# A cross-attention and expert layer: keys and values ahead of the queries, LayerNorm's constants as two-tensor operations

## What is computed

```python
def _layernorm(x, eps=1e-05):
    m, v = jnp.mean(x, -1, keepdims=True), jnp.var(x, -1, keepdims=True)
    return (x - m) / jnp.sqrt(v + eps)

# cross-attention, 16 heads of 32
q = _layernorm(x) @ Wq + bq
k, v = ctx @ Wk + bk, ctx @ Wv + bv
x = x + softmax(q k^T * SCALE) v @ Wo + bo
# (causal self-attention whose values have width HD - ROPE = 0: it adds nothing)
# expert layer: top 2 of 8 experts for each of the 512 tokens
x = x + moe(_layernorm(x))
```

## Time and profile before

| what | value |
|---|---|
| time, median of 3 runs | 1229.38 us (1228.88 to 1230.99) |
| profiled execution, its own time | 1227.9 us |
| its span, first to last instruction | 1226.1 us |
| mean granted TensorE clock | 0.97 |
| TensorE products busy | 1143.8 us, 93% of the span |
| VectorE busy | 958.2 us, 78% |
| ScalarE busy | 704.6 us, 57% |
| GpSimd busy | 428.0 us, 35% |

### The profile page before, as it was taken

How to read it: one execution, slowest core, us unless ns; L and a number is a source line. 1 busy time by engine, 2 the same in 40 slices (tenths; PEclk the granted TensorE clock), 3 DMA queues, 4 the chain that set the end, 5 groups by cost and what they waited for, 6 DMA issues and landing times.

```text
span 1226.1 us, 23151 instructions
## 1 busy us (share of the span) xinstructions
PE 1143.8 (93%) x7488; PEld 1054.2 (86%) x7489; DVE 958.2 (78%) x2082; ACT 704.6 (57%) x1418; POOL 428.0 (35%) x378
## 2 busy tenths in 40 slices
PE   4899999999999999999999998757889999889998
PEld 4799999999999999999999997635668898668897
DVE  6578888888888888888888888865876756876655
ACT  3456656656656656656656656443575565665654
POOL 5454754754654654654664640010000000000000
PEclk9899999999999999999999999966899999989999
DMA  5322122122122122122122103113755634655633
GB/s 181 101 63 62 40 70 61 38 70 61 38 70 61 38 70 61 38 70 61 39 69 61 58 23 118 50 52 105 244 189 184 206 109 164 221 191 193 201 117 103
DMA packets 74304, 121.15 MB, mean 99 GB/s; under 512 B 10776, under 2 KB 35480, under 8 KB 74272
## 3 DMA queue, kind: packets, MB, share of 16 engines
q1 hardware_dynamic: 74272, 120.73, 30.6%
HBM read 118.62 MB, written 2.10 MB: 98 GB/s over the span
## 4 chain that ended last, share of the span: by engine, by line
PE 79%; DVE 9%; ACT 5%; DMA 3%; issue 3%; DVEq 0%; SPq 0%; ACTq 0%
PE ps L401 18%; PE ps L403 17%; PE ps L402 17%; PE ps L1285 7%; PE ps L1337 7%; PE ps L1321 4%; PE ps L1322 3%; DMA w_raw<-in_w_dram 2%; PE ps L1386 2%; DVE w_lo L1027 2%; DVE mx L955 1%; DVE k_mix L877 1%; PE ps L1429 1%; DVE w_lo L1019 1%; PE ps L1430 1%
## 5 line engine op out<-in xcount | busy, mean ns | idle before, releaser
L545 POOL TENSOR_TENSOR ctx_hi<-ctx_raw,no_query 128x1152 fp32r<-128x1152 f32 x64 | 142.8, 2231 | 290.2 <-PE ps L403 281.2
L877 DVE SCALAR_TENSOR_TENSOR k_mix<-ps,bk_sb,k_mix 64x384 fp32r<-64x384 f32 (+1 forms) x256 | 162.3, 634 | 82.1 <-ACT k_mix L644 77.8
L684 ACT ACTIVATE probs<-ps,negmax 128x1152 f32<-128x1152 f32 x64 | 78.3, 1223 | 201.1 <-DVE negmax L958 201.1
L401 PE MATMUL ps<-wv_hi,ctx_hi 128*128 128x256 f32 (+1 forms) x624 | 181.8, 291 | 6.7 <-DVE k_mix L877 6.5
L549 POOL TENSOR_TENSOR ctx_lo<-ctx_raw,ctx_hi 128x1152 fp32r<-128x1152 f32 x64 | 179.7, 2808 | 5.0
L403 PE MATMUL ps<-wv_hi,ctx_lo 128*128 128x256 f32 (+1 forms) x624 | 175.7, 282 | 0.0
L402 PE MATMUL ps<-wv_lo,ctx_hi 128*128 128x256 f32 (+1 forms) x624 | 174.9, 280 | 0.0
L644 ACT ACTIVATE k_mix<-ps,bk_sb 64x384 fp32r<-64x384 f32 (+1 forms) x256 | 150.8, 589 | 24.0 <-PE ps L403 19.4
L969 DVE TENSOR_TENSOR pt_mix<-ps,pt_mix 128x384 fp32r<-128x384 f32 (+1 forms) x256 | 142.2, 580 | 1.4 <-ACT pt_mix L695 1.4
L401 PE MATMUL ps<-ctx_hi,wk_hi 128*128 128x384 f32 (+1 forms) x384 | 133.2, 347 | 0.0
L403 PE MATMUL ps<-ctx_hi,wk_lo 128*128 128x384 f32 (+1 forms) x384 | 132.3, 345 | 0.0
(11 more groups left out here) (219 smaller groups left out, 2668.5 us busy)
## 6 DMA issues: line engine op xcount, KB each, us to landing
w_raw<-in_w_dram SPq DMA_DIRECT2D x68, 1024.0 KB, 5.3
ctx_raw<-in_ctx_t_dram SPq DMA_DIRECT2D x48, 576.0 KB, 3.8
ctx_raw<-in_ctx_t_dram SPq DMA_DIRECT2D x16, 673.5 KB, 4.1
q_both<-q_scratch SPq DMA_DIRECT2D x14, 128.0 KB, 3.1
x<-in_x_dram SPq DMA_DIRECT2D x1, 1024.0 KB, 5.4
wq_raw<-in_wq_dram SPq DMA_DIRECT2D x1, 1024.0 KB, 7.7
q_scratch<-q_out SPq DMA_DIRECT2D x1, 1024.0 KB, 5.4
wo_raw<-in_wo_dram SPq DMA_DIRECT2D x1, 1024.0 KB, 5.4
```

The source lines that it names most:

```text
L401: pe.matmul(acc_ap, a_hi, b_hi, start=start, stop=False)
L545: nc.gpsimd.tensor_tensor(ctx_hi[slot][:, :, 0:n], ctx_raw[slot][:, :, 0:n], no_query[:].rearrange("p (o i) -> p o i", o=1).broadcast_to([ ...
L877: last = nc.vector.scalar_tensor_tensor(out=k_mix[other, 2 * a + i, cols], in0=ps[rows, bank, 0:m], scalar=bk_sb[rows, a:a + 1], in1=k_mix ...
```

## The change

1. **Order of the opening.** SP issues the three biases first, then wk and ctx chunk 0 in three slices of the contraction (128 rows of wk, the same 128 of ctx), then wv, x, ctx chunk 1, wq. ScalarE and VectorE split each slice as it comes, and unit 0 starts with its first slice (`by_parts`). TensorE does all units of chunks 0 and 1 (0 to 9), then the transposes of xn0, then the queries, then units 10 to 20.
2. **Who splits.** ctx chunk 0: ScalarE high, VectorE low; chunk 1: ScalarE high, GpSimd low; wq_lo moves from VectorE to GpSimd.
3. **LayerNorm in pieces** between the units' halves on VectorE: statistics after unit 0, variance after unit 1, inverse after unit 4, normal rows in two pairs after units 5 and 6. ScalarE waits for the variance between its key and value halves of chunk 0, and splits wq before the halves of chunk 1.
4. **LayerNorm's arithmetic**, in both LayerNorms: eps added from a tile; the factor 0.5 replaced by doubling the reciprocal; `tensor_scalar` on the rows replaced by `scalar_tensor_tensor` with rstd spread over the columns.
5. **First queries** are placed by groups of heads: group 0 under the query products, groups 1 to 3 in pairs of blocks between the halves of chunk 2 (ScalarE) and chunk 3 (VectorE). The store of the queries goes behind two loads of ctx in SP's queue. SBUF is laid out anew to suit.

```diff
+            sp.dma_start(bk_sb[:], bk_t).then_inc(bias_loaded, 16)
+            sp.dma_start(bq_sb[:], bq_t).then_inc(bias_loaded, 16)
+            sp.dma_start(bv_sb[:], bv_t).then_inc(bias_loaded, 16)
+            for k in range(KC):
+                sp.dma_start(wkv_raw[:, 0, k, :], wk[k * P:(k + 1) * P, :]).then_inc(first_loaded[k], 16)
+                sp.dma_start(ctx_raw[0][:, k, 0:KEYS[0]], ctx_view[0, :, k, 0:KEYS[0]]
+                             ).then_inc(first_loaded[k] if k < KC - 1 else ctx_loaded[0], 16)
+            sp.dma_start(wkv_raw[:, 1], wv.rearrange("(k p) n -> p k n", p=P)).then_inc(wv_loaded, 16)
             sp.dma_start(x0[:], x_rows).then_inc(x_loaded, 16)
+            load_ctx(0, 1, 1)
             sp.dma_start(wq_raw[:], wq.rearrange("(k p) n -> p k n", p=P)).then_inc(wq_loaded, 16)
...
             make_norm_tables()
-            for m in range(CHUNKS):
-                split_ctx(m + 1, m, 16 * (m // 2 + 1), UNIT0[m - 1] if m >= 2 else None)
+            pool.wait_ge(ctx_high, 2)
+            pool.wait_ge(ctx_split, 1)
+            nc.gpsimd.tensor_tensor(ctx_lo[1][:, :, 0:KEYS[1]], ctx_raw[1][:, :, 0:KEYS[1]],
+                                    ctx_hi[1][:, :, 0:KEYS[1]].bitcast(F32), ALU.subtract).then_inc(ctx_split, 1)
+            pool.wait_ge(wq_high, 1)
+            nc.gpsimd.tensor_tensor(wq_lo[:], wq_raw[:], wq_hi[:].bitcast(F32), ALU.subtract).then_inc(wq_split, 1)
+            for m in range(2, CHUNKS):
+                split_ctx(m + 1, m, 16 * (m // 2 + 1), UNIT0[m - 1])
...
+            split_first(wkv_raw[:, 1], wv_hi[:], wv_loaded).then_inc(wkv_high, 1)
+            split_first(ctx_raw[1][:, :, 0:KEYS[1]], ctx_hi[1][:, :, 0:KEYS[1]], ctx_loaded[1]).then_inc(ctx_high, 1)
...
             act.wait_ge(bias_loaded, 48)
+            job_high(None, 0, range(len(KEY_UNITS)))
+            act.wait_ge(var_ready, 1)
+            nc.scalar.activation(sd[:], ve[:], ACT.Sqrt).then_inc(sd_ready, 1)
+            warm(ACT.Exp, 1)
+            job_high(None, 0, range(len(KEY_UNITS), UNITS[0]))
+            split_first(wq_raw[:], wq_hi[:], wq_loaded).then_inc(wq_high, 1)
+            job_high(None, 1, range(UNITS[1]))
...
+            for c in range(2, CHUNKS):
+                for k in range(UNITS[c]):
+                    job_high(None, c, [k])
+                    if c == 2 and k < HPG:
+                        for i in (2 * k, 2 * k + 1):
+                            src, to, pairs, cols = first_queries(i, 1, GROUPS)
+                            last = nc.scalar.copy(qbd_hi[to, pairs, cols], q_out[src, 1:GROUPS, 0:NQ])
...
-                    nc.vector.tensor_scalar(dst[:, t, :], src[:, t, :], mv[:, t, 0:1], rstd[:, t:t + 1],
-                                            ALU.subtract, ALU.mult).then_inc(xn_ready, 1)
+            def normal_rows(src, dst, tiles):
+                for t in tiles:
+                    nc.vector.scalar_tensor_tensor(out=dst[:, t, :], in0=src[:, t, :], scalar=mv[:, t, 0:1],
+                                                   in1=rstd[:, t:t + 1].broadcast_to([P, D]), op0=ALU.subtract,
+                                                   op1=ALU.mult).then_inc(xn_ready, 1)
...
+            job_low(None, 0, KEY_UNITS[:1])
+            dve.wait_ge(x_loaded, 16)
+            for t in range(TT):
+                last = nc.vector.bn_stats(stat[:, t, :], x0[:, t, :])
+            step(last)
+            job_low(None, 0, KEY_UNITS[1:])
+            variance()
+            job_low(None, 0, range(len(KEY_UNITS), UNITS[0]))
+            inverse_deviation(1)
+            job_low(None, 1, KEY_UNITS[:1])
+            normal_rows(x0, xn0, range(2))
+            job_low(None, 1, KEY_UNITS[1:])
+            normal_rows(x0, xn0, range(2, TT))
+            job_low(None, 1, range(len(KEY_UNITS), UNITS[1]))
...
+            project(units_of(CHUNKS)[0], 0, PROJ_BANK, by_parts=True)
+            for c in range(2):
+                for k in range(UNITS[c]):
+                    if c > 0 or k > 0:
+                        pe.wait_ge(wkv_split, KC if k in KEY_UNITS else KC + 1)
+                        run_job(None, c, [k])
+            turn(xn0, 0, TT)
+            pe.wait_ge(wq_split, 1)
+            pe.wait_ge(xt_split, KD)
+            pe.wait_ge(proj_split, UNIT0[2])
```

More of the change, by code:

```diff
@@ new lines, in _ @@
+            dve.wait_ge(pv_taken, 1)
+            dve.sem_inc(pv_free, 1)
+            dve.wait_ge(tables_ready, 5)
+            for c in range(2, CHUNKS):
+                for k in range(UNITS[c]):
+                    job_low(None, c, [k])
+                    if c == CHUNKS - 1 and k < HPG:
+                        dve.wait_ge(qbd_high, GROUPS)
+                        for i in (2 * k, 2 * k + 1):
+                            src, to, pairs, cols = first_queries(i, 1, GROUPS)
+                            last = nc.vector.tensor_tensor(qbd_lo[to, pairs, cols], q_out[src, 1:GROUPS, 0:NQ],
@@ L1234, in _, with project @@
             pe.wait_ge(psum_zeroed, 1)
-            turn(xn0, 0, TT)
-            pe.wait_ge(wq_split, 1)
-            pe.wait_ge(xt_split, KD)
-            for m in range(KD):
-                for k in range(KD):
-                    last = three_pass(pe, ps[:, 4 + m, :], wq_hi[:, k, m * P:(m + 1) * P], wq_lo[:, k, m * P:(m + 1) * P],
-                                      xt0_hi[:, k, :], xt0_lo[:, k, :], k == 0, k == KD - 1)
-                last.then_inc(q_ready, 1)
-            def project(unit, n, bank):
+            def project(unit, n, bank, by_parts=False):
                 kind, a, c = unit
                 for k in range(KC):
+                    if by_parts:
+                        pe.wait_ge(wkv_split, k + 1)
+                        if k < KC - 1:
+                            pe.wait_ge(first_split, k + 1)
+                        else:
+                            pe.wait_ge(ctx_split, 1)
                     if kind == "keys":
```

173 lines of the change are left out of this document (93 added, 80 removed).

## The result

The changed kernel takes 1240.04 us (median of 4 runs, 1238.67 to 1240.23) against 1230.18 (median of 4, 1228.88 to 1231.02) for the kernel before: a ratio of 1.0079, 95% interval 1.0061 to 1.0096. It is slower by 9.9 us. A second set, four runs of the changed kernel beside 17 of the one before, gave 1240.56 (1236.12 to 1242.51) and a ratio of 1.0091 (1.0072 to 1.0111). The forecast was 1237.9, 8.5 us slower.

The account below looks back on a forecast made before the run. TensorE, busy for 93% of the span, was taken as the bound. Terms 6.2 + 1.4 + 0.9 = +8.5 us on the median 1229.4 gave 1237.9 us, with an 8-in-10 range of 1230.5 to 1243.

Parts of the forecast that it names:

- The chain of the opening: Opening, from chunk 1's landing through ScalarE, VectorE and GpSimd to the queries: unit 10 starts at 57.0 against 50.78, +6.2 us.
- Rival C: Opening: no turns, and ctx chunk 1 lands up to 3.8 us sooner because transfers share engines; faster, 1227.0; chance 0.10.
- The turns: Opening: VectorE's SBUF-only rows and GpSimd's operations block each other for whole instructions, so transposes start only at 39.1.
- A: Opening: the forecast itself, normal rows wait for GpSimd; ends at 1237.9, bounds 1233.5 to 1242; chance 0.73.
- B: Opening: spread rstd is no second stream, no turns, transposes at 34.0; about the same time, 1230.8; chance 0.13.
- The rows now have two inputs: Opening, VectorE's normal rows: inputs x0 and the spread rstd, given as the reason they take turns with GpSimd.
- The low clock over the first queries: Query products after TensorE's pause: half clock for about 4 us loses 1.9 us, counted within the +6.2.
- Chunks 2 and 3: From unit 10 to the first exponential: placing pairs of queries there costs +1.4 us, bounds 0.4 and 2.0.
- the pair behind unit 18 meets GpSimd's next split: Chunk 3 on VectorE: the 2.11 us split delays the last low halves, the maxima and the first exponential.
- The second LayerNorm: Normal rows there, which TensorE waits for: two-tensor form takes about 2.8 us for four against 1.92, +0.9 us.
- the constants: LayerNorm's eps and 0.5: two operations on four columns exchanged for two others, costing nothing.

Follow-up runs that it names:

- experiment 1: Changed kernel, but GpSimd begins its splits of chunk 2 only when all four normal rows are done; one run took 1235.12 us.
- experiment 5: Changed kernel, but GpSimd waits ahead of its first batch until all first queries are placed; one run took 1238.19 us.
- experiment 8: Changed kernel with chunk 0's key halves before chunk 1's split, GpSimd's splits after the rows, `tensor_scalar` rows, GpSimd's loop after query placement; 1229.53 us, ratio 0.9992.
- experiment 11: Changed kernel with GpSimd's wq_lo in four pieces and both operations of its splits of chunks 2 and 3 in three each; one run took 1236.34 us.
- experiment 3: Changed kernel with the rows of both LayerNorms made by the one-tensor `tensor_scalar` again; one run took 1235.50 us.
- experiment 2: Changed kernel, but both GpSimd's wq_lo and its splits from chunk 2 on wait for the four normal rows; 1237.14 us, ratio 1.0047.
- experiment 6: Kernel before, with first queries placed in pairs behind units of chunk 2 (ScalarE) and chunk 3 (VectorE); 1227.54 us, ratio 0.9970.
- experiment 7: Kernel before, with first queries placed in pairs, VectorE's pairs ahead of units of chunk 3 instead of behind; 1226.79 us, ratio 0.9972.
- experiment 9: Kernel before, with first queries placed in pairs behind units of chunks 2 and 3, and GpSimd's batch loop waiting for the placed queries; 1226.55 us, ratio 0.9970.

## Why the prediction was right, and where it was not

The direction, the mechanism and, within 1.4 us, the size held. Its steps, in us from the start:

| step | forecast | measured |
|---|---|---|
| first product of unit 0 | 7.5 | 7.30 |
| split of ctx chunk 1 starts | 14.9 | 15.99 |
| statistics start | 18.5 | 19.60 |
| variance written | 22.9 | 23.96 |
| wq_lo on GpSimd | 27.7 to 32.3 | 28.53 to 33.12 |
| low half of unit 5 starts | 28.8 | 31.11 |
| row 1 ends | 35.4 | 36.18 |
| low half of unit 6 ends | 36.7 | 37.47 |
| transposes start | 39.1 | 39.93 |
| first query product | 44.2 | 44.91 |
| unit 10 | 57.0 (+6.2) | 56.10 (+5.3) |
| unit 10 to first exponential, more than before | +1.4 | +3.35 |
| rows of the second LayerNorm, more than before | +0.9 | +0.8 |
| whole | +8.5 | +9.9 |

- **The chain of the opening** stood as written, about 1 us late from the landing of chunk 1 on and 0.7 at its end. Rival C is out: that chunk didn't come early. One wait was missing: ScalarE's halves of unit 5 waited 1.39 for TensorE, which ran at 0.50 from 20 to 28 after its stalls. It cost nothing, since row 0 had to wait for wq_lo in any case. Units 0 to 2 also ended at 16.6 and not by 15, since they ran mostly at the low level (below); that cost nothing either, as unit 3 had to wait for its bank until 19.72.
- **The turns** The earlier trace rows decided, as A had it and B had not. Experiments 1, 5, 8 and 11 show it by taking GpSimd away and by shortening its pieces. The reason given was only half right: "The rows now have two inputs" holds, but it is not what brought the turns, since experiment 3's rows, with one tensor, wait too. What brought them is that GpSimd works beside the rows.
- **The low clock over the first queries**, 1.9 us, did not come: 48 products took 11.2, not 12.8. The clock had fallen in the pause as said, but it was back at 44, just as they began. The size was right where it did occur (1.6 in experiments 2 and 8). Such a term is a chance, not a sum.
- **Chunks 2 and 3** is the term that was mis-sized: +3.35, outside its bounds of 0.4 and 2.0. The scores came 1.0 later (0.5 was forecast), and behind them the first exponential 5.58 after the scores instead of 3.24. The mechanism is the one named, "the pair behind unit 18 meets GpSimd's next split":

```profile
73.12 2.53 DVE L1005 TENSOR_TENSOR qbd_lo<-q_out,qbd_hi 32x192 fp32r<-32x192 f32 x2
```

  The pair takes 2.53, not 0.71, and the low halves of units 19 and 20 and the maxima stand behind it. The delay in front of the scores and the collision behind them come one after the other, and I had taken one middle value for both. Experiments 5 and 8 give 1.8 of the 3.35 to the collision (from unit 10 to the first exponential experiment 8 takes 69.91 - 49.22 = 20.69, the changed kernel 22.55, the one before 19.20); that the other 1.5 are the pairs' own time on VectorE and the wait for banks is argued from the order, not shown by a run.
- **The second LayerNorm**: 746 ns a row, 0.8 in all; experiments 3 and 8, with 1.92 for four, confirm it from the other side. That the constants cost nothing was not tried alone.
- The errors cancelled in part: -0.9 in front of unit 10, +1.95 behind it.

**What the change did bring.** Placing the queries in pairs is worth 3 to 4 us by itself (experiments 6, 7, 9). The rest of the change costs 78.65 - 67.34 = 11.3 us at the first exponential, against experiment 6. Experiment 8 takes 8.7 of it back and still has the keys and values first; it stands 2.6 behind experiment 6, of which 1.6 are the low clock over its queries. Against experiment 9, which has the same wait on GpSimd and lost about as much to the low clock over its queries (1.5), it stands 3.1 behind. So even without the turns and the wait for chunk 1, the new order brought nothing that the first exponential shows. TensorE begins 7 us earlier, but until the queries it is granted 0.50 for some 17 us between 18 and 44 (the windows' shortfall from 1.00, doubled), goes at that level before 16 as well (below), and stands still for 12 in six pieces, most of them waits for VectorE's low halves.

**The spread between executions.** In the profiles of experiments 7 and 9 the first query products, in the order of before, followed each other at 0.43 us until 22 to 23 us, at 0.23 only then; in experiment 6 and in the kernel before it was 0.23 from the first on. This is of experiment 7:

```profile
20.07 0.63 PE L403 MATMUL ps<-xt_hi,wq_lo 128*128 128x512 f32 x1
20.49 0.63 PE L401 MATMUL ps<-xt_hi,wq_hi 128*128 128x512 f32 x1
...
23.03 0.40 PE L401 MATMUL ps<-xt_hi,wq_hi 128*128 128x512 f32 x1
23.27 0.40 PE L402 MATMUL ps<-xt_lo,wq_hi 128*128 128x512 f32 x1
```

It costs 1.5 to 1.9 us when it occurs, and may be a part of the 5.6 us between the fastest and the slowest run of the kernel before. The window of 20 to 22 records a clock of 1.00 for it. That record can't be read before its first change: in the changed kernel, too, it is 1.00 from the start, while the 384 columns of unit 0 follow each other at 0.32 us, as those of unit 5 do in the window of 26 to 28, recorded at 0.50 (1.2 GHz; at 1.00 it is 0.17), and 256 columns at 0.12 after 15.9:

```profile
12.23 0.52 PE L412 MATMUL ps<-ctx_lo,wk_hi 128*128 128x384 f32 x1
12.55 0.52 PE L413 MATMUL ps<-ctx_hi,wk_lo 128*128 128x384 f32 x1
...
15.99 0.28 PE L413 MATMUL ps<-wv_hi,ctx_lo 128*128 128x256 f32 x1
16.11 0.28 PE L411 MATMUL ps<-wv_hi,ctx_hi 128*128 128x256 f32 x1
```

So the program starts at the low level and leaves it near 16 in the one order, and in the other by 19 in some executions and at 22 to 23 in others, by the spacing of the products. What sets the moment stays open, as does the part of the tail (the experts' blocks) in the 9.9 us: 1.7 in one profile, none in the next.

## What to carry to other kernels

When work is handed from VectorE to GpSimd, list VectorE's operations that lie wholly in SBUF in the time when GpSimd is busy, and price each at the rest of the GpSimd instruction it meets; the low halves, with an input in PSUM, were free of that here. A block of small operations in an in-order queue is best spread behind the units that wait for nothing, but check every slot against GpSimd's timeline, since moving it by one unit only moved the wait (0.6 us gained in the profile, nothing that the times show). That starting the bounding engine earlier pays only if the engines that feed it have less to do before it can go on is how I read experiment 8; no run tried the new order with less work on them.
